# Two transformer layers on one core: pairs of heads share a half of the rows, score units of two pairs alternate, and the logits follow the second layer's last unit

## The reference, cut to what matters

```python
xn = layernorm(x)
# layer 0
h = rmsnorm(xn); q, k, v = h @ Wq, h @ Wk, h @ Wv           # 16 heads of 8
lin = (1 + s + s*s/2 of causal q_phi, k_phi) v / row sums    # scores s of (q Wqf, k Wkf)
win = softmax(q k / sqrt(8), causal, window of 64) v
x1 = x + xn + concat(lin, win) @ Wout + ffn(xn)              # silu gate, two gelu layers of 512, w3
# layer 1
xn = layernorm(x1); h = xn * gamma + beta
q, k, v = h @ Wq + bq, h @ Wk + bk, h @ Wv + bv
out = x1 + softmax(q k / sqrt(8), causal) v @ Wo + bo
      + sum over the top 2 of 8 experts, by softmax of xn @ Wg.T
```

## Time and profile before

| | |
|---|---|
| median of 3 runs | 1283.01 us (1282.63 to 1283.72) |
| profiled execution | 1290.89 us, span 1289.1 us |
| PE busy | 1165.4 us (90%) |
| DVE busy | 865.2 us (67%) |
| ACT busy | 743.5 us (58%) |
| POOL busy | 649.6 us (50%) |
| mean granted TensorE clock | 0.965 |
| chain that ended last, by engine | PE 49%, DVE 21%, ACT 13%, issue 8%, POOL 6% |

### The profile page before, as it was taken

How to read it: one execution, slowest core, us unless ns; L and a number is a source line. 1 busy time by engine, 2 the same in 40 slices (tenths; PEclk the granted TensorE clock), 3 DMA queues, 4 the chain that set the end, 5 groups by cost and what they waited for, 6 DMA issues and landing times.

```text
span 1289.1 us, 26679 instructions
## 1 busy us (share of the span) xinstructions
PE 1165.4 (90%) x9122; PEld 750.8 (58%) x9122; DVE 865.2 (67%) x3433; ACT 743.5 (58%) x1580; POOL 649.6 (50%) x846
## 2 busy tenths in 40 slices
PE   5989999999999899989998999899989867988997
PEld 2445754565457545754575457545764456884896
DVE  4066588658865885688658865786578755885563
ACT  2356367735773577457745774477546624557675
POOL 4475254535444454545454544454445436675577
PEclk9998999999999899999999999899989969999999
DMA  7601620162015301540154015401472016542233
GB/s 237 153 3 54 177 73 12 54 184 73 13 55 147 108 15 39 151 120 15 39 152 117 17 39 151 117 17 39 139 211 64 5 26 142 82 70 29 41 55 40
DMA packets 123961, 105.53 MB, mean 82 GB/s; under 512 B 15242, under 2 KB 118578, under 8 KB 123826
## 3 DMA queue, kind: packets, MB, share of 16 engines
q1 hardware_dynamic: 102162, 85.89, 24.7%
q0 software_dynamic: 13792, 9.54, 5.1%
q10 hardware_dynamic: 7872, 8.39, 1.9%
HBM read 58.59 MB, written 46.37 MB: 81 GB/s over the span
## 4 chain that ended last, share of the span: by engine, by line
PE 49%; DVE 21%; ACT 13%; issue 8%; POOL 6%; DMA 2%; DVEq 0%; SPq 0%; POOLq 0%; ACTq 0%
PE bank L700 14%; PE heads L765 11%; ACT probs L1117 8%; PE bank L679 6%; PE bank L707 6%; DVE xnT_s L1585 4%; DVE hrow L1585 4%; DVE hT_s L1585 3%; POOL out L1362 3%; PE bank L690 2%; PE bank L675 2%; DVE spare L1585 2%; PE bank L1050 2%; PE bank L684 1%; PE bank L815 1%
## 5 line engine op out<-in xcount | busy, mean ns | idle before, releaser
L1117 ACT ACTIVATE probs<-bank 128x512 f32<-128x512 f32 (+2 forms) x896 | 441.2, 582 | 176.6 <-PE bank L707 169.8
L1309 POOL TENSOR_SCALAR_AFFINE_SELECT probs<-probs 128x384 f32<-128x384 f32 x256 | 127.7, 521 | 242.1 <-ACT probs L1117 242.1
L765 PE MATMUL heads<-probs,V 128*18 128x192 f32 (+9 forms) x3072 | 194.6, 394 | 10.7 <-POOL probs L1312 4.6
L707 PE MATMUL bank<-K,Q 128*128 128x192 bf16 (+4 forms) x1024 | 199.2, 271 | 4.3 <-ACT probs L1117 0.2
L707 PE MATMUL bank<-Q,K 128*128 128x192 bf16 (+4 forms) x1024 | 175.0, 275 | 16.3 <-ACT probs L1117 7.0
L1362 POOL DMA_INDIRECT out<-h1T_s x78 | 123.2, 1580 | 60.3 <-ACT h1T_s L1270 37.4
L765 PEld LDWEIGHTS heads<-probs,V 128*9 128x9 f32 (+1 forms) x3072 | 78.2, 94 | 122.3 <-issue 85.4
L1262 ACT ACTIVATE h2T_s<-bank,h1T_s 128x128 f32<-128x128 f32 x312 | 89.2, 368 | 93.1 <-PE bank L1050 80.9
L707 PEld LDWEIGHTS bank<-Q,K 128*128 128x128 bf16 x1024 | 81.4, 99 | 87.5 <-ACT probs L1117 31.1
L707 PE MATMUL bank<-QM,K 128*128 128x512 bf16 (+3 forms) x512 | 121.5, 301 | 7.8 <-DVE gatesT_s L1545 1.4
L707 PEld LDWEIGHTS bank<-K,Q 128*128 128x128 bf16 x1024 | 85.2, 98 | 67.7 <-DVE mx_c L1585 14.3
(11 more groups left out here) (241 smaller groups left out, 2285.1 us busy)
## 6 DMA issues: line engine op xcount, KB each, us to landing
K<-slots_of_k SPq DMA_DIRECT2D x64, 256.0 KB, 4.2
Q<-slots_of_q SPq DMA_DIRECT2D x15, 1024.0 KB, 10.9
QM<-slots_of_qm SPq DMA_DIRECT2D x8, 1024.0 KB, 9.4
h1T_s<-sorted_rows SPq DMA_DIRECT2D x78, 65.0 KB
slots_of_q<-Q SPq DMA_DIRECT2D x8, 384.0 KB, 2.6
slots_of_k<-QM SPq DMA_DIRECT2D x8, 384.0 KB, 2.9
slots_of_qm<-Q SPq DMA_DIRECT2D x8, 384.0 KB, 2.6
slots_of_k<-Q SPq DMA_DIRECT2D x8, 384.0 KB
```

Source lines behind the costliest of these rows:

```text
L707: mm = pe.matmul(to[:, at:at + right.shape[1]], left, right, start=True, stop=True, skip_group_check=True)
L765: mm = pe.matmul(heads[ROWS * i:ROWS * i + n, P * j:P * j + widths[j]], V[:, j, g // 2, i, first:first + n], slot_of(kind, 2 * g + i // 2) ...
L1117: return act.activation(to, bank, func, scale=scale, bias=bias).then_inc(taken_sem(run, unit), 1)
L1309: pool.affine_select(out=three, in_=three, compare_op=ALU.is_ge, fill=0.0, base=0, pattern=[[0, 3], [1, P]], channel_multiplier=-1)
```

## The change

Nothing of what is computed changes. Three things do.

**Rows.** All score products, but cmax in the tail, are over 64 rows: keys and queries are sliced to the half that the head owns (`own(h)`), and the zero rows are no longer read.

**Pairs and units.** A pair is now heads h and h+2, both in the same half of the rows, so a group of four heads has one pair in the upper half and one in the lower. The units of the two pairs alternate: `a` of the one, `a` of the other, `b`, `b`, and the two `_` units come last in each ten. Where linear and causal scores begin with one half, cmax begins with the other (`HALVES`). A pair's last unit is unit 8 or 9 of its ten (`last_tri`), where it was unit 4 or 9, and of a sliding group of eight it is 6 or 7 (`last_slide`), where it was 3 or 7. ACT's slots, DVE's maxima and middle masks and POOL's masks follow.

**Logits.** In the dense stage the unit `h2_3` (12 products) comes ahead of the logits, not behind.

```diff
+HALVES = {"lin": (0, 1), "causal": (0, 1), "cmax": (1, 0)}
+def heads_of(p):
+    first = HG * (p // 2) + p % 2
+    return first, first + 2
+def tri_unit(tag, n):
+    g, r = n // (2 * 5), n % (2 * 5)
+    i = HALVES[tag][r % 2]
+    return ("_", 2 * g + i) if r >= 8 else ("ab"[r % 4 // 2], HG * g + 2 * (r // 4) + i)
+def slide_unit(n):
+    r = n % 8
+    return "ab"[r % 4 // 2], HG * (n // 8) + 2 * (r // 4) + r % 2
+def last_tri(p):
+    return 2 * 5 * (p // 2) + 8 + p % 2
+def last_slide(p):
+    return 8 * (p // 2) + 6 + p % 2
...
+            def own(h):
+                return slice(SROWS * (h % SH), SROWS * (h % SH + 1))
-            def q_part(buf, h, a, n):
-                return buf[:, h // SH, a:a + n]
+            def q_part(buf, h, a, n, rows):
+                return buf[rows, h // SH, a:a + n]
...
-                    return at, keys[:, h, P * j:P * (j + 1)], q_part(buf, h, P * j, TRI_N[j])
+                    return at, keys[own(h), h, P * j:P * (j + 1)], q_part(buf, h, P * j, TRI_N[j], own(h))
...
+                    rows = slice(0, P) if run[0] == "tail" else own(h)
+                    return at, q_part(Q2, h, P * j, P, rows), K2b[rows, h, 0:P * (j + 1)]
...
-                        at = head * (i % 2) + starts[j]
+                        at = head * (i // 2) + starts[j]
                         mm = pe.matmul(heads[ROWS * i:ROWS * i + n, P * j:P * j + widths[j]],
-                                       V[:, j, g // 2, i, first:first + n], slot_of(kind, 2 * g + i // 2)[:, at:at + widths[j]],
+                                       V[:, j, g // 2, i, first:first + n], slot_of(kind, 2 * g + i % 2)[:, at:at + widths[j]],
...
                 project_rows(run, "v2", hT, wv1[:, :])
+                if after:
+                    dense_low(run, "h2_3", layer2, 3)
                 wait_taken(run, "xnT2")
                 project_rows(run, "logits", xnT, wgT[:, :], E)
-                if after:
-                    dense_low(run, "h2_3", layer2, 3)
-                else:
+                if not after:
                     run_tiles(QUERIED, ROUTED)
...
-                last_unit = units[5 * p + 4]
+                last_unit = units[last_tri(p)]
                 pool.wait_ge(taken_sem(run, last_unit), taken_at(run, last_unit))
...
-                last_unit = SLIDE_UNITS[4 * p + 3]
+                last_unit = SLIDE_UNITS[last_slide(p)]
...
-                    if n % 4 == 2 and n > 2 and this:
-                        mask_middle(run, n // 4 - 1)
+                    if n % 8 in (1, 3) and n > 8 and this:
+                        mask_middle(run, 2 * (n // 8 - 1) + n % 8 // 2)
...
                 if this:
+                    mask_middle(run, H // 2 - 2)
                     mask_middle(run, H // 2 - 1)
```

More of the change, by code:

```diff
@@ L175, in dense_order @@
     units += ["h2_2"] if after else []
-    units += ["hT2", "k2", "q2", "xnT2", "v2", "logits"] if this else []
+    units += ["hT2", "k2", "q2", "xnT2", "v2"] if this else []
     units += ["h2_3"] if after else []
+    units += ["logits"] if this else []
     return units
@@ L1161, in causal_stage @@
                     if before:
-                        slot = pair_slot(previous, CAUSAL, n // 5, (LIN, now)) if n % 5 == 0 else slot_of(CAUSAL, n // 5)
-                        tri_unit(run, CAUSAL_UNITS, slot, n, ACT.Exp, SCALE, 0.0)
+                        if n % 10 == 0:
+                            wait_slots(previous, CAUSAL, n // 10, (LIN, now))
+                        tri_probs(run, CAUSAL, CAUSAL_UNITS, n, ACT.Exp, SCALE, 0.0)
                     if n == 9:
@@ L1588, in slide_max @@
             def slide_max(run, n):
-                h = n // 2
+                half, h = slide_unit(n)
                 def part(j, at):
```

92 lines of the change are left out of this document (45 added, 47 removed).

## The result

The changed kernel took 1387.97 us (median of four runs, 1372.27 to 1389.37), against 1283.32 for the kernel before beside it: ratio 1.0788 [1.071, 1.0866]. The forecast was 1310 us with a range of 1264 to 1346: the sign was right, and the time lies outside the range. The profiled execution took 1387.21 us (span 1385.5, mean granted clock 0.902; before 0.965).

A forecast was written before the change was run, and what follows sets the result against it. The prediction took DVE's maxima plus the weighings to bound the pairs stage, with POOL pacing the seam behind. Its terms, -12.8 - 5.6 + 23.4 + 7 + 3 + 12 = +27.0, gave a median of about 1310 us, range 1264 to 1346.

The forecast's parts named there:

- 23.4 + 7 + 3 + 12: Added microseconds: late masks in six steady batches, in the first batch, in last batch and tail, and lower clock behind hrow's wait.
- Score products over 64 rows, -5.6 us: Score products in two halves overlap: nothing gained in the pairs stage, 0.8 us in each of seven sliding stages.
- the ring: Pairs stage: PE is held between weighings by seven banks that DVE's maxima free, so faster score products gain nothing.
- That rival: Pairs stage: overlap shrinks PE's work, the clock falls, three of seven weighings lose 2 us: 42 us, 1352 us; chance 0.17.
- its own sign: Pairs stage: a granted clock of 0.50 between two weighings of most stages would decide for the clock-falls case.
- The other two rivals: POOL's masks keep up, 1265 us, chance 0.22; or 64-row halves do not overlap, 1316 us, chance 0.08.
- Logits, -12.8 us: Dense stage, seven batches: h2_3 covers PE's 2.41 us wait for xnT; DVE regains 14.9 us less 7 x 0.3.
- the bound of 0: Logits' move: no gain if DVE's later wait for the third layer grows by as much; other bound -27 us.
- Masks at the end of the pairs stage: Mask of causal pair 6 falls behind the third causal weighing, delaying hrow and the next weighing: 2.8 us in six batches.
- First batch, +7 us: First batch: POOL's other work falls between the two masks of a group, delaying weighings by 0 to 11.4 us.
- The clock behind the new wait, +12: Ahead of hT1 PE idles about 3 us and the clock falls: six times about 2 us, 0 to 20 in all.

The follow-up runs named there:

- the same-half run: Changed kernel with cmax's HALVES set to (0, 1), so a product and the maximum next to it share a half: 1377.5 us, ratio 1.0635.
- the second run: Kernel before with only the logits moved behind the second layer's last unit, measured again on another chip: 1279.5 us, ratio 0.9976.
- The early power: Changed kernel with POOL's two norm powers ahead of causal pair 6's mask: 1357.8 us, 1.0486; with all score products over 128 rows too: 1322.5 us, 1.0215.
- the edit there: 128 rows, powers ahead, first-batch POOL work behind odd masks (1307.4 us), plus DVE's middle sliding mask moved next to the division: 1296.9 us, ratio 1.0118.
- the 128-row kernel: Changed kernel with every score product over all 128 rows again, new order, masks and logits' place kept: 1342.0 us, ratio 1.0374.

## Why the prediction was wrong

The sum said +27.0 us; between the profiled executions it was +96.3. Of the 69 us between them, 47 are the rows (41.7 instead of -5.6), 20 are order and masks (65.5 instead of 23.4 + 7 + 3 + 12 = 45.4) and 2 the logits.

- **Score products over 64 rows, -5.6 us: the step that failed.** "In the pairs stage the ring holds PE, so nothing" was right for the length of a stretch (8.3 and 8.4 us, with 64 and with 128 rows) and for the overlap of halves. The term counted only what such a product takes, and left out what it does to the clock of the weighings behind: +41.7 us of span was the result. That rival stood in the text with a chance of 0.17, and by its own sign, a granted 0.50 between the weighings of most stages, it is the one that came. Its 42 us are near the 41.7 by luck: it counted 3 slow weighings in 7 at 2 us each, and in the six steady batches 12 of 42 are slow and cost 17 us. Nor is its reason shown: it had PE's shrunken work between the weighings, and the same-half run lost the clock with PE busy for 7.80 of 8.30 us. What is shown is that 64 rows in the new order cost the clock and that added products keep it; what it is in them, and why the old order was spared, stays open. How much of the 41.7 us is clock is not shown either. As an estimate: the changed kernel's eight executions grow by some 7.6 us for each 0.01 of mean clock, and the two kernels differ by 0.047 (0.949 and 0.902), which gives some 36 us. The other two rivals are out: halves overlap, and mask 6 did start late.
- **The rival was held against one row only.** For it the text had a stretch with PE busy for 1.05 of 3.4 us, and nothing nearer to the case. A stretch busy for 2.16 of 3.40 us lost the clock too.
- **Logits, -12.8 us: near in the profiled execution, too large in the median.** The wait for xnT went from 19.1 to 1.8 us in the changed kernel, but PE now waits 24.9 us for DVE's sliding maxima, where it was 1.8. The spans say -10.9 for the logits alone, the medians 3 us. The execution on which the sum was made lay 7.9 us above its median, and 10.9 less 7.9 is 3: differences were carried over unscaled from an execution that long. Which waits made it longer was not looked at. The reason given for the bound of 0, a later wait for the third layer, was the right one: 1.71 us and, in the second run, 2.05 to 2.44, instead of 1.06.
- **Masks at the end of the pairs stage: right.** The mask of pair 6 starts 3.86 us behind the start of the third causal weighing (before: 1.0, with that weighing at 619.5), and hrow costs PE 3.73 us where 2.8 more than before was said. The early power took back 19.5 us with 128 rows; the prediction had 6 x 2.8 and 12 for the clock behind it, 28.8, but of the wait 1.55 us stayed in each batch, for the mask of pair 7.
- **First batch, +7 us: 21 measured** (18.9 against -2.1 for the logits alone). Of the changed kernel's four rows above, 11.1 us are waits, as bounded (11.4), and 8.1 are the weighings at the lower clock behind them, which the text left out.
- **End of the sliding stage: a missing term.** 0.7 us more of wait and 1.6 of clock, seven times, would be 16 us; the edit there gave back 10.5.
- **The clock behind the new wait, +12**, was right in kind but stood for one place. It also came at the first batch's weighings and the first hidden layer and, behind the wait that the logits' move made, at the third layer (5.2 to 5.7 us instead of 3.74).

## What to carry to other kernels

Where buffers and not PE set the pace, a faster product buys nothing and may cost the clock of the next PE-bound stretch. Neither the lack of long gaps nor a high busy share of PE is a sign that the clock will hold: read the granted clock, and the time of one group of products that recurs. Bound every added wait of PE by the wait and the slow products behind it, in each place where it occurs. When a gain is read from one profiled execution that lies above its median, scale it down or take it from several executions.

## What the runs showed of the hardware

- The granted clock fell to 0.50 with no PE wait over 0.31 us, behind 3.4 us in which PE was busy for 2.16; in the same place of the 128-row kernel, with 3.23, it stayed at 1.00.
- PE's busy time in the profile does not tell whether the clock holds: between the same two weighings, 7.80 us of 8.30 in the same-half run ended in a weighing of 4.04 us, and 7.69 of 8.60 with some 64-row products issued twice in one of 2.34.
- Redundant products made a kernel 1.2% faster (1.0674 against 1.0799, on one chip).
- A wait of 3.73 us ahead of PE's products made the weighing behind take 4.44 us instead of 2.34; one of 1.55 us just ahead of the same weighing left it at 2.34.
- The same kernel before took 1282 to 1283 us on some chips and 1295 to 1297 on others, with mean granted clocks of 0.97 and 0.96, while the kernel with the logits moved took 1279.5 and 1280.1. A small gain measured on one chip can be four times that on another. The changed kernel took 1373.9 to 1393.1 us in four executions on one chip, with mean clocks of 0.917 to 0.892.
